# The order of an attention body: where TensorE issues values, keys and value sums, and which engine empties the projected values

## What is computed

```
q = split_heads(layernorm(x) @ Wq.T + bq)        # x: 16 batches, 64 tokens, 128 wide
k = split_heads(ctx @ Wk.T + bk)                 # ctx: 16 batches, 1601 rows, 128 wide
v = split_heads(ctx @ Wv.T + bv)                 # 16 heads of 8
weights = softmax(q k.T / sqrt(8))
x = x + (weights @ v) @ Wo.T + bo
```

## Time and profile before

| | |
|---|---|
| median of 3 runs | 572.72 us (571.77 to 573.69) |
| the profiled execution's own time | 574.46 us |
| its span on the core | 572.6 us |
| TensorE matmul / weight load busy | 520.9 us (91%) / 338.6 us (59%) |
| VectorE / ScalarE / GpSimd busy | 419.7 us (73%) / 380.4 us (66%) / 323.6 us (57%) |
| mean granted TensorE clock | 0.976 |

### The profile page before, as it was taken

How to read it: one execution, slowest core, us unless ns; L and a number is a source line. 1 busy time by engine, 2 the same in 40 slices (tenths; PEclk the granted TensorE clock), 3 DMA queues, 4 the chain that set the end, 5 groups by cost and what they waited for, 6 DMA issues and landing times. The chain is left out here.

```text
span 572.6 us, 18926 instructions
## 1 busy us (share of the span) xinstructions
PE 520.9 (91%) x7882; PEld 338.6 (59%) x7882; DVE 419.7 (73%) x749; ACT 380.4 (66%) x704; POOL 323.6 (57%) x197
## 2 busy tenths in 40 slices
PE   3887999999999999999999999999999869999997
PEld 1534565565565565565565565665375736777776
DVE  6287888797797798788788799447877567455554
ACT  4883668678678678778778778873844426656662
POOL 1698878558558558558657299204000035667673
PEclk9897999999999999999999999999989979999999
DMA  6776444354354354354352463002000000000001
GB/s 210 137 154 132 124 112 96 91 119 93 87 121 96 81 120 97 83 119 98 81 119 49 107 145 84 3 2 101 2 1 2 1 1 1 2 2 0 0 0 38
DMA packets 17962, 41.64 MB, mean 73 GB/s; under 512 B 5542, under 2 KB 8366, under 8 KB 17770
## 3 DMA queue, kind: packets, MB, share of 16 engines
q1 hardware_dynamic: 17144, 40.10, 30.2%
q10 hardware_dynamic: 740, 0.42, 0.2%
HBM read 19.70 MB, written 0.52 MB: 35 GB/s over the span
## 5 line engine op out<-in xcount | busy, mean ns | idle before, releaser
L911 DVE TENSOR_REDUCE half_max<-wide 128x2 f32<-128x802 f32 x256 | 241.6, 988 | 42.8 <-PE wide L596 38.8
L836 ACT ACTIVATE probs<-score 128x512 f32<-128x512 f32 (+1 forms) x416 | 225.8, 596 | 66.6 <-PE score L647 66.3
L667 PE MATMUL sums<-probs,values 128*32 128x192 f32 (+3 forms) x3328 | 131.6, 280 | 0.0
L667 PEld LDWEIGHTS sums<-probs,values 128*32 128x32 f32 (+1 forms) x3328 | 86.9, 110 | 51.4 <-issue 22.6
L596 PE MATMUL wide<-k_stack,q_cur 48*128 48x401 bf16 x512 | 87.5, 339 | 12.6 <-ACT k_full L818 6.2
L647 PE MATMUL score<-q_cur,k_stack 50*128 50x128 bf16 (+1 forms) x1664 | 82.7, 219 | 7.3 <-ACT probs L836 6.3
L425 POOL TENSOR_TENSOR ctx_hi<-ctx_in,one 128x1601 bf16<-128x1601 f32 x15 | 42.9, 2857 | 76.9 <-PE wide L517 67.8
L1904 POOL TENSOR_TENSOR hid_lo<-hid_e,hid_hi 114x512 bf16<-114x512 f32 x47 | 54.1, 1156 | 35.5 <-ACT hid_hi L1928 34.3
L647 PEld LDWEIGHTS score<-q_cur,k_stack 50*128 50x128 bf16 (+1 forms) x1664 | 51.9, 95 | 32.7 <-ACT probs L836 12.9
L2039 DVE SCALAR_TENSOR_TENSOR hid_e<-gu,keep_bgu,gate 114x512 f32<-114x512 f32 x48 | 35.9, 750 | 40.1 <-ACT gate L1941 40.0
L438 POOL TENSOR_TENSOR k_hi<-k_full,one 128x1601 bf16<-128x1601 f32 x15 | 42.8, 2856 | 31.0 <-ACT k_full L818 24.9
(11 more groups left out here) (327 smaller groups left out, 919.1 us busy)
## 6 DMA issues: line engine op xcount, KB each, us to landing
k_stack<-k_hi SPq DMA_DIRECT2D x128, 102.0 KB, 3.4
ctx_in<-in_ctx SPq DMA_DIRECT2D x56, 200.1 KB, 3.4
k_stack<-k_lo SPq DMA_DIRECT2D x64, 102.0 KB, 3.2
ctx_in<-in_wgu SPq DMA_DIRECT2D x16, 171.0 KB, 3.4
keep_w<-in_w SPq DMA_DIRECT2D x1, 1368.0 KB
ctx_in<-in_ctx SPq DMA_DIRECT2D x1, 800.5 KB, 8.4
keep_x<-in_x SPq DMA_DIRECT2D x1, 512.0 KB, 7.0
q_cur<-shift SPq DMA_DIRECT2D x30, 2.0 KB
```

Source lines behind the costliest of these rows:

```text
L667: last = pe.matmul(sums[32 * g:32 * g + 32, first * LQ:(first + heads) * LQ], values[0:m, n, k, VW * g + 2 * c:VW * g + 2 * c + 32], probs ...
L836: nc.scalar.activation(probs[0:m, step % NPROB, :].rearrange("r (g p c) -> r p g c", g=G, p=2)[:, p], score[0:m, (2 * step + p) % NSCORE, ...
L911: dve.tensor_reduce(half_max[:, b % 2, :, u // 4, u % 4], wide[:, w, :].rearrange("p (c k) -> p c k", c=2)[:, :, 0:CH], AX.X, ALU.max).the ...
```

## The change

TensorE's order within a body is written anew, and ScalarE instead of VectorE empties the values of batches 3 to 15 (those made in the loop).

- Both halves of the values are issued back to back in step 3; ScalarE copies them after the exponentials of step 3, behind a wait for the sums of the batch that held the slot before.
- The keys' halves stand in steps 7 and 8. The first is issued ahead of the step's maxima, and ScalarE empties it between the two exponentials of step 7; the second is issued after the first maxima of step 8 and emptied after the step's exponentials.
- The sums 0 and 1 stand in step 4, 2 and 3 in step 5, 4 to 12 in steps 6, 7, 9, 10, 11, 12 and in steps 0, 1, 2 of the next body. In steps 1, 2, 5, 6 and 11 they stand ahead of the maxima. ScalarE copies `sums` out in step 2 in place of step 1. After the last body three sums follow in place of two.
- The maxima of batches 3 and up stand by a written list: none in steps 3 and 9, three in step 4, two in steps 0, 8 and 10, one elsewhere.

```diff
-LEAD = 5
-V_STEPS, K_STEPS = (2, 5), (6, 8)
+V_STEP, K_STEPS = 3, (7, 8)
+UNIT_STEPS = (8, 10, 10, 11, 12, 13, 13, 14, 15, 17, 17, 17, 18, 19, 20, 21)
+SUM_STEPS = (4, 4, 5, 5, 6, 7, 9, 10, 11, 12, 13, 14, 15)
+SUMS_BEFORE_MAXIMA = (1, 2, 5, 6, 11)
...
+def sums_at(i, k):
+    return [(b, s) for b in (i - 1, i) if b >= 0 for s in range(NK) if NK * (b - i) + SUM_STEPS[s] == k]
...
-    return kind == "x" or kind == "k" and b > 0
+    return kind == "x" or kind == "k" and b > 0 or kind == "v" and b > 2
...
                     scores(i, k)
                     units = units_at(i, k)
+                    for b, half in keys_at(i, k):
+                        if half == 0:
+                            keys(b, half)
+                    if k in SUMS_BEFORE_MAXIMA:
+                        for b, s in sums_at(i, k):
+                            sum_values(b, s)
                     if units:
                         maxima(*units[0])
-                    if i >= 1 and k < 2:
-                        sum_values(i - 1, NK - 2 + k)
-                    if k == 3:
-                        sum_values(i, 0)
-                    if k >= 3:
-                        sum_values(i, k - 2)
-                    if k in V_STEPS and 0 < i < B - 2:
-                        vals(i + 2, V_STEPS.index(k))
-                    for half in keys_at(i, k):
-                        keys(*half)
+                    if k == V_STEP and 0 < i < B - 2:
+                        for half in range(2):
+                            vals(i + 2, half)
+                    for b, half in keys_at(i, k):
+                        if half == 1:
+                            keys(b, half)
+                    if k not in SUMS_BEFORE_MAXIMA:
+                        for b, s in sums_at(i, k):
+                            sum_values(b, s)
                     for unit in units[1:]:
                         maxima(*unit)
...
+            sum_values(B - 1, NK - 3)
             sum_values(B - 1, NK - 2)
             sum_values(B - 1, NK - 1)
...
+            def vals_out(b, half):
+                w, nk = filled(act, ("v", b, half)), 7 - half
+                if half == 0:
+                    act.wait_ge(s_pv, NK * (b - NSLOT + 1))
+                src = wide[:, w, 0:P * nk].rearrange("p (k g c) -> p k g c", k=nk, g=G)
+                dst = values[:, b % NSLOT, 7 * half:7 * half + nk, :].rearrange("p k (g c) -> p k g c", g=G)
+                nc.scalar.copy(dst[:, :, :, 1:VW - 1], src).then_inc(s_by_act, 1)
...
-                    if i >= 1 and k == 1:
-                        sums_out(i - 1)
-                    for half in keys_at(i, k):
-                        keys_out(*half)
+                        if i >= 1 and k == 2 and p == 1:
+                            sums_out(i - 1)
+                        if k == V_STEP and 0 < i < B - 2 and p == 1:
+                            for half in range(2):
+                                vals_out(i + 2, half)
+                        for b, half in keys_at(i, k):
+                            if half == p:
+                                keys_out(b, half)
...
-                    if k in V_STEPS and 0 < i < B - 2:
-                        vals_out(i + 2, V_STEPS.index(k))
```

More of the change, by code:

```diff
@@ L60, in units_at @@
     for b in (i + 1, i + 2):
-        lead = {1: 0, 2: 3}.get(b, LEAD)
-        found += [(b, u) for u in range(16) if 1 <= b < B and
-                  NK * (b - 1) - lead + (lead + 8) * u // 16 == NK * i + k]
-    return found
+        lead = {1: 0, 2: 3}.get(b)
+        found += [(b, u) for u in range(16) if 1 <= b < B and NK * i + k == (
+            NK * (b - 2) + UNIT_STEPS[u] if lead is None else NK * (b - 1) - lead + (lead + 8) * u // 16)]
+    return found
+def sums_at(i, k):
+    return [(b, s) for b in (i - 1, i) if b >= 0 for s in range(NK) if NK * (b - i) + SUM_STEPS[s] == k]
 def keys_at(i, k):
@@ L105, in ring_order @@
         for k in range(NK):
+            order += [("k",) + half for half in keys_at(i, k) if half[1] == 0]
             order += [("m",) + unit for unit in units_at(i, k)[:1]]
-            if k in V_STEPS and 0 < i < B - 2:
-                order += [("v", i + 2, V_STEPS.index(k))]
-            order += [("k",) + half for half in keys_at(i, k)]
+            if k == V_STEP and 0 < i < B - 2:
+                order += [("v", i + 2, half) for half in range(2)]
+            order += [("k",) + half for half in keys_at(i, k) if half[1] == 1]
             order += [("m",) + unit for unit in units_at(i, k)[1:]]
@@ L902, in vals_out @@
                 w, nk = filled(dve, ("v", b, half)), 7 - half
-                if half == 0 and b >= NSLOT:
-                    dve.wait_ge(s_pv, NK * (b - NSLOT + 1))
                 src = wide[:, w, 0:P * nk].rearrange("p (k g c) -> p k g c", k=nk, g=G)
```

## The result

| | before | changed |
|---|---|---|
| median | 573.21 us (571.77 to 574.86, 4 runs) | 556.41 us (554.75 to 557.11, 4 runs) |
| ratio | | 0.9708, 95% interval 0.9687 to 0.9729 |
| profiled execution / its span | 574.46 / 572.6 us | 556.66 / 554.6 us |
| attention stage, from the first scores of body 0 to the first matmul behind the stage | 337.5 us (49.35 to 386.86) | 321.2 us (50.38 to 371.55) |

What follows compares the result with a forecast made beforehand. TensorE's own work was taken as nine tenths of the bound, only its waits winnable. Gains 16.9 + 1.9 + 0.3, less 0.65, 0.5 and 0.45, make 17.5 us: from 572.72 to 555.2 us, range 549.5 to 565.

Steps and rivals of the forecast that it cites:

- TensorE's waits are what can be won: Bodies 2 to 12, walked: 19.2 us of work plus 0.6 of waits, 19.81 a body for 21.35.
- The term of 16.9 us: Forecast gain of the eleven steady bodies, 2 to 12: 11 x 1.54 us.
- With sums ahead of maxima ... nothing is won.: Order within a step: TensorE's 0.26 becomes 0.18 but 0.24 becomes 0.33, so its own work gains nothing.
- ScalarE's copies, 1.03 and 0.89 us: Emptying the values' halves, 896 and 768 columns, priced by the column from ScalarE's 802-column emptying of the keys.
- The shift's copies, SyncE and GpSimd hide: Shift's copies start 2.86 us ahead of the scores needing them (2.62 before); GpSimd's split starts earlier; no wait claimed.
- Body 1, 1.9 less: Body 1, with two maxima round the values and a later step 4: 22.95 to 21.0 us, 1.2 over the walk.
- Body 0, nothing: Body 0 is set by VectorE, with two maxima a step; no change claimed.
- (1) VectorE starves: Handovers of `wide` in steps 4 to 12 cost more than walked, 0.8 us a body: about 565 us; chance 0.14.
- (2): Steps 3 to 4: ScalarE's value copies cost by small piece, delaying step 5's scores: 576 to 577 us; chance 0.05.
- (3): Waits only move to the next body's scores, because the shift's copies land late: no change (572); chance 0.03.
- (4): All 0.6 us of waits a body vanish too, leaving 19.2 us: 548 us; chance 0.06.
- three signs of being wrong: Copies over 1.3 us; exponentials waiting for sums beyond step 4; TensorE waits of 0.5 us for VectorE in steps 10 to 12.

Runs made afterwards that it cites:

- maxima_first: The changed kernel with the maxima ahead of the sums in every step: 569.16 us, 0.9935 of the kernel before.
- order_only: The changed kernel's new order, but VectorE still empties all values: 559.57 us, 0.9777 of the kernel before.
- maxima_spread_evenly: The changed kernel with the earlier even list of maxima for batches 3 and up: 589.33 us, 1.0277 of the kernel before.
- batch2_by_list: The changed kernel with batch 2's maxima also by the written list, from step 8 of body 0: 552.08 us, 0.9644 of the kernel before.
- engine_only: The kernel before, old order kept, with ScalarE in place of VectorE emptying the values of batches 3 to 15: 569.95 us, 0.9951 of the kernel before.
- old_sums_at_ends: The changed kernel with the old steps of the sums for batches 0, 14 and 15: 554.78 us, 0.9703 of the kernel before.

## Why the prediction was right, point by point

- **TensorE's waits are what can be won, 19.2 us of work under a body.** Shown: 19.69 measured, 19.81 walked, and each step within 0.11. The term of 16.9 us was 18.2 (234.80 - 216.63). The missing 0.12 a body is the wait in step 12, 0.11 and not 0.23. It comes from one edge of the walk: turned maxima to the next reduction, taken as 1.35, was 1.22 (193.48 - 192.26). In the kernel before VectorE was still reducing when the turned maxima came (until 199.57, 197.49 + 2.08; turned at 198.93), so the 1.35 had a wait of the old order in it.
- **"With sums ahead of maxima ... nothing is won."** True of TensorE's own time and wrong as a reading of the change: by maxima_first the same pieces in the other order within the step cost 1.26 us a body more, three quarters of the gain. The walk had this in it, since it used the new order; the sentence did not.
- **ScalarE's copies, 1.03 and 0.89 us.** Measured 0.91 and 0.80. The Trainium skill (ScalarE: Activation LUTs, "What ACT_TABLE_LOAD costs") gave by its formula an estimate of 0.93 and 0.83, within 4% of the rows and nearer than my price by the column. Its table "Rules for kernel authors" sends relu, max, min, add and mul to VectorE. Copies are not in it; by the same rule they would have stayed there, which costs 0.27 us a body (order_only), so this case doesn't bear the rule out for fp32 copies.
- **The shift's copies, SyncE and GpSimd hide.** Right: TensorE shows no wait for the shift in body 6, and GpSimd's work, 13.4 us a body, is unchanged.
- **Body 1, 1.9 less.** This term failed: 22.81 after 22.95, where 21.0 was put. The walk gave 1.2 us to its two maxima round the values. Between the `sums` copies the body is 2.9 us over a steady one, 2.0 of it in steps 3 and 4. The part that was guessed in place of walked is that the maxima of step 3 and the values' first half each wait for VectorE (0.33 and 0.56 us), which has four reductions in a row. maxima_spread_evenly shows the same wait, batch2_by_list removes it.
- **Body 0, nothing.** This term failed too: 25.88 for 25.06. The growth lies in steps 5 and 6, 4.23 us for 3.24, where a second pair of sums now stands beside maxima that wait for VectorE; steps 3 and 4 together take 5.01 for 4.99. The mean granted clock was 0.87 (the last window above) against 0.93 in that window of the kernel before, but that explains little: engine_only, whose body 0 is that of the kernel before, had 0.86 and took 24.08 us from the first scores to those of body 1, for 23.98 before and 24.80 after. That the late sums cause it is borne out by old_sums_at_ends, with 23.66 there.
- **Body 13, 0.3 less; body 14, 0.65 more; body 15 and the end, 0.95 more.** Measured 0.44 less, 1.16 more, 0.43 more (from 350.91 to 371.55 after, 366.65 to 386.86 before). The signs hold, two of the sizes are off by a factor of about two.
- **The sum.** The stage's terms give 18.2 + 0.1 + 0.4 - 1.2 - 0.4 - 0.8 = 16.3 us, against 17.5 forecast. The steady bodies gave 1.3 us more than forecast, and bodies 0, 1 and 14 together 3.1 less, bodies 13 and 15 0.7 more, so the total is nearer than its terms, and in part by luck. The profile's span fell by 18.0. The rest lies outside the stage: its first scores came 1.0 us later, and the untouched stages behind it took 183.1 us for 185.7. In the kernel before two stretches of those ran at a mean clock of 0.92 (400 to 420 and 440 to 462 us), after the change at 1.00. Over all fourteen profiles here the first scores lie between 47.9 and 50.4 us, and the tail between 182.5 and 185.8, with no order by the change. So of the profile's 18.0 us only 16.3 are the change, and the stage ended 15.3 us earlier, not 17. The medians differ by 16.8.
- **Rivals.** (1) VectorE starves: no, 19.69 a body; but maxima_first shows the price of such a place, 0.8 us in one step. (2) No; its chain exists, its price was too high. (3) No. (4) No: waits remain, 19.69 us a body and not 19.2. None of the three signs of being wrong showed in body 6: the copies are under 1.3 us, one exponential alone waits for sums (0.37), and the wait for VectorE in step 12 is 0.11.

## What to carry to other kernels

When a few kinds of work share a double buffer, write down for each step who takes a half and who empties it, and put work that needs no half between two takers. Here that placement made 589 or 556 us out of the same instructions. Walk one period with start-to-start distances from the trace, the bodies at the edges too: the steady body came out within 0.6%, and the larger errors for a single body, up to 1.8 us, were where I had put a guess in place of the walk.

## What the runs showed of the hardware

- Cutting a ScalarE copy into small pieces costs less than the length of a piece says: 13 copies of 128 columns at 335 ns each are busy 2.31 us in a body, 0.18 apart, and 26 copies of 64 columns at 372 ns each 3.12 us, 0.12 apart; whole copies 1.71.
- A matmul group on all rows of the array starts 0.08 to 0.09 us later behind a group on fewer rows than another group on fewer rows does (maxima to sums 0.26, maxima to scores 0.18; scores to sums 0.33, scores to maxima 0.24), the same in both kernels within 0.01.
- The same program can differ by about 1 us in one body with TensorE's granted clock: a step with two sums and two maxima took 2.79 us with the clock at 0.50 for most of it and 2.07 with it mostly at full (step 5 of body 0, maxima_spread_evenly and the changed kernel).
- The untouched stages behind the attention differ by up to 3 us between profiles, and most where they differ in the time that TensorE's granted clock stood at its lower level in them: about 7 us in the seven profiles with 182.5 to 183.3 us, 10 to 14 us in the seven with 184.3 to 185.8. So a single pair of spans can't tell a change of 0.5%.
